# Two attention stages cut into 24 blocks of 128 destinations and one of 53, with one transfer per store

## The reference, cut to what matters

```python
h = (x @ W).reshape(n, heads, out_ch)
al_s, al_d = einsum('nhc,hc->nh', h, a_src), einsum('nhc,hc->nh', h, a_dst)
e = leaky_relu(al_s[src] + al_d[dst], 0.2)
ee = exp(e - segment_max(e, dst)[dst])
alpha = ee / (segment_sum(ee, dst)[dst] + 1e-16)
out = segment_sum(h[src] * alpha[:, :, None], dst) + b
```

## Time and profile before

| | us |
|---|---|
| median of 3 runs | 3902.7 (3895.01 to 3902.9) |
| the profiled execution, as a run | 3902.42 |
| its span, first to last instruction | 3900.3 |
| TensorE matmul busy | 3489.8 (89%) |
| TensorE weight load busy | 3228.9 (83%) |
| VectorE busy | 2067.2 (53%) |
| ScalarE busy | 1702.6 (44%) |
| GpSimd busy | 231.6 (6%) |
| line 1866 in g1a, first and last start | 1938.3 and 2512.5 |
| line 1866 in g2a, first and last start | 2668.7 and 3242.9 |

### The profile page before, as it was taken

One profiled execution on the slowest core, in us unless ns is written; L12 is line 12 of the kernel. 1 busy time (PEld: TensorE's weight loads), 2 busy tenths in 40 slices (PEclk: granted clock), 3 DMA queues, 4 the chain that ended last, 5 costly groups with the idle time before them and its releaser, 6 DMA issues. The chain is left out here.

```text
span 3900.3 us, 65697 instructions
## 1 busy us (share of the span) xinstructions
PE 3489.8 (89%) x27372; PEld 3228.9 (83%) x27372; DVE 2067.2 (53%) x2212; ACT 1702.6 (44%) x1945; POOL 231.6 (6%) x320
## 2 busy tenths in 40 slices
PE   3888889999956999878699999788999996899899
PEld 3568879999956999745599999778999996899676
DVE  6665556666653222364367667514667663466421
ACT  0444445555523434232155555414555552455332
POOL 1000000000001222100101001100011001000000
PEclk9879989999967999889799999999999998999979
DMA  3213365655525655501256555324556553654020
GB/s 110 56 33 49 52 139 150 161 159 143 143 78 173 203 188 178 161 15 32 70 150 170 146 163 154 89 80 130 145 163 170 140 153 86 161 138 137 14 56 27
DMA packets 184563, 464.88 MB, mean 119 GB/s; under 512 B 73944, under 2 KB 106465, under 8 KB 182777
## 3 DMA queue, kind: packets, MB, share of 16 engines
q1 hardware_dynamic: 166984, 424.31, 40.0%
q0 software_dynamic: 13904, 33.84, 2.8%
q10 hardware_dynamic: 3399, 2.76, 0.2%
HBM read 407.32 MB, written 53.50 MB: 118 GB/s over the span
## 5 line engine op out<-in xcount | busy, mean ns | idle before, releaser
L1866 PE MATMUL g2a_ps<-HX,g2a_x 125*125 125x129 f32 (+2 forms) x5200 | 574.5, 273 | 7.8 <-DVE g2a_x L1742 7.8
L1866 PE MATMUL g1a_ps<-HX,g1a_x 125*125 125x129 f32 (+2 forms) x5200 | 574.5, 273 | 7.8 <-DVE g1a_x L1742 7.8
L1866 PEld LDWEIGHTS g2a_ps<-HX,g2a_x 125*125 125x125 f32 x5200 | 574.3, 188 | 8.0 <-issue 8.0
L1866 PEld LDWEIGHTS g1a_ps<-HX,g1a_x 125*125 125x125 f32 x5200 | 574.3, 188 | 8.0 <-issue 8.0
L1866 PE MATMUL g0a_ps<-HX,g0a_x 125*125 125x122 f32 x5000 | 548.3, 273 | 7.9 <-DVE g0a_x L1742 7.9
L1866 PEld LDWEIGHTS g0a_ps<-HX,g0a_x 125*125 125x125 f32 x5000 | 548.1, 190 | 8.0 <-issue 8.0
L1742 DVE SCALAR_TENSOR_TENSOR g2a_x<-g2a_x,g2a_flat,g2a_ct 125x3125 f32<-125x3125 f32 x100 | 347.3, 3475 | 188.2 <-ACT g2a_x L1794 188.2
L1742 DVE SCALAR_TENSOR_TENSOR g1a_x<-g1a_x,g1a_flat,g1a_ct 125x3125 f32<-125x3125 f32 x100 | 347.3, 3474 | 188.1 <-ACT g1a_x L1794 188.1
L1742 DVE SCALAR_TENSOR_TENSOR g0a_x<-g0a_x,g0a_flat,HX 125x3125 f32<-125x3125 f32 x100 | 347.3, 3475 | 180.2 <-ACT g0a_x L1794 180.2
L1794 ACT ACTIVATE g2a_x<-g2a_grow,g2a_minus,g2a_steep 125x3125 f32<-125x3125 f32 x100 | 299.3, 2995 | 248.3 <-PE g2a_ps L1866 248.3
L1794 ACT ACTIVATE g1a_x<-g1a_grow,g1a_minus,g1a_steep 125x3125 f32<-125x3125 f32 x100 | 299.3, 2995 | 248.3 <-PE g1a_ps L1866 248.2
(11 more groups left out here) (577 smaller groups left out, 3897.0 us busy)
## 6 DMA issues: line engine op xcount, KB each, us to landing
HX<-counted SPq DMA_DIRECT2D x150, 683.6 KB
g1a_ct<-counted SPq DMA_DIRECT2D x100, 683.6 KB
g2a_ct<-counted SPq DMA_DIRECT2D x100, 683.6 KB
moe_wa<-in_L_ffn_W SPq DMA_DIRECT2D x56, 1024.0 KB
counted<-HX SPq DMA_DIRECT2D x12, 1367.2 KB
HX<-counted SPq DMA_DIRECT2D x150, 79.3 KB
g1a_ct<-counted SPq DMA_DIRECT2D x100, 79.3 KB
g2a_ct<-counted SPq DMA_DIRECT2D x100, 79.3 KB
```

Source lines behind the costliest of these rows:

```text
L1866: done = nc.tensor.matmul(ps[0:R, bank, col:col + f1 - f0], x[:, n % XR, t * R:(t + 1) * R], whole_row[:, sb, h0 + f0:h0 + f1], start=(sb ...
```

## The change

In the two stages with output "elu" the destinations are cut into 24 blocks of 128 and one of 53 (24 x 128 + 53 = 3125) in place of 25 of 125. The sources stay in 25 blocks of 125. So a weight load has 128 columns in 24 of 25 blocks, and 53 in the last; the number of matmuls and the moving operand stay. `D_` is the block's size and `rows(t)` the number of destinations in block t. The last block, the one whose columns are split over banks 0 and 1, becomes a chunk of its own for `divide`, `elu`, `lower` and the store (ND = 9 chunks, while the banks and the moves stay at CH = 8); all other chunks have three blocks. The buffers `y` and `low` hold three blocks in place of four. Each store is one transfer of 128 partitions (53 for the last chunk) in place of two of 112 and 13 partitions, so 9 x 4 = 36 transfers in a stage. The buffer `wide` is renamed `span`, because `wide` now is the flag. In the stages g0a and g3a nothing changes.

```diff
-    tiles = [range(per * c, per * c + per if c < CH - 1 else T) for c in range(CH)]
-    most = 4
+    wide = g.out == "elu"
+    D_, ND = (P, CH + 1) if wide else (R, CH)
+    tiles = [range(per * c, T if c == ND - 1 else per * c + per) for c in range(ND)]
+    most = 3 if wide else 4
...
-        raw, rec = s.sb("raw", [R, T, F + 1]), s.sb("rec", [R, T])
-        y = s.sb("y", [R, YR, most, F])
+        raw, rec = s.sb("raw", [D_, T, F + 1]), s.sb("rec", [D_, T])
+        y = s.sb("y", [D_, YR, most, F])
...
+        def rows(t):
+            return min(D_, N - D_ * t)
...
-                for n in range(G * CH):
-                    gr, c = n // CH, n % CH
-                    t0, t1 = tiles[c][0], tiles[c][-1] + 1
+                for n in range(G * ND):
+                    gr, c = n // ND, n % ND
+                    t0, t1, p = tiles[c][0], tiles[c][-1] + 1, rows(tiles[c][0])
                     pool.wait_ge(y_ready, n + 1)
-                    tile_dma(pool, OUT[t0 * R:t1 * R, gr * F:(gr + 1) * F].rearrange("(t p) f -> p t f", p=R), y[:, n % YR, 0:t1 - t0, :], y_out[n % YR])
+                    pool.dma_start(OUT[t0 * P:t0 * P + p * (t1 - t0), gr * F:(gr + 1) * F].rearrange("(t p) f -> p t f", p=p), y[0:p, n % YR, 0:t1 - t0, :]).then_inc(y_out[n % YR], 16)
                 for k in range(YR):
-                    pool.wait_ge(y_out[k], 32 * (G * CH // YR))
+                    pool.wait_ge(y_out[k], 16 * (G * ND // YR))
...
-                dve.wait_ge(moved, n + 1)
+                dve.wait_ge(moved, gr * CH + min(c + 1, CH))
...
-            for n in range(NU + XR + CH + 2):
+            for n in range(NU + XR + ND + 2):
...
-                done = nc.scalar.activation(raw[:, t0:t0 + n, :], ps[0:R, bank, 0:n * W].rearrange("p (t w) -> p t w", t=n)[:, :, b0:b0 + F + 1], ACT.Copy)
+                done = nc.scalar.activation(raw[:, t0:t0 + n, :], ps[0:D_, bank, 0:n * W].rearrange("p (t w) -> p t w", t=n)[:, :, b0:b0 + F + 1], ACT.Copy)
                 for t, col, f0, f1 in found[n:]:
-                    done = nc.scalar.activation(raw[:, t, f0:f1], ps[0:R, bank, col:col + f1 - f0], ACT.Copy)
+                    p = rows(t)
+                    done = nc.scalar.activation(raw[0:p, t, f0:f1], ps[0:p, bank, col:col + f1 - f0], ACT.Copy)
...
-                        done = nc.tensor.matmul(ps[0:R, bank, col:col + f1 - f0], x[:, n % XR, t * R:(t + 1) * R], whole_row[:, sb, h0 + f0:h0 + f1],
+                        done = nc.tensor.matmul(ps[0:rows(t), bank, col:col + f1 - f0], x[:, n % XR, t * D_:t * D_ + rows(t)], whole_row[:, sb, h0 + f0:h0 + f1],
```

More of the change, by code:

```diff
@@ L1630, in stage_gat_sums @@
             ct = spare.bitcast(BF16).rearrange("p (k n) -> p k n", k=CR)
-        raw, rec = s.sb("raw", [R, T, F + 1]), s.sb("rec", [R, T])
-        y = s.sb("y", [R, YR, most, F])
+        raw, rec = s.sb("raw", [D_, T, F + 1]), s.sb("rec", [D_, T])
+        y = s.sb("y", [D_, YR, most, F])
         if g.out == "elu":
-            low = s.sb("low", [R, 2, most, F])
+            low = s.sb("low", [D_, 2, most, F])
         ends, least, both = s.sb("ends", [R, 2 * S]), s.sb("least", [R, S]), s.sb("both", [R, 2 * S])
         end, diag, middle = s.sb("end", [2 * S, 1]), s.sb("diag", [2 * S, 2 * S]), s.sb("middle", [R, S])
-        wide, under = s.sb("wide", [1, S]), s.sb("under", [R, 1])
+        span, under = s.sb("wide", [1, S]), s.sb("under", [R, 1])
         near, far = s.sb("near", [R, S, T]), s.sb("far", [R, S, T])
@@ L1724, in prepare @@
                 nc.vector.tensor_tensor(middle[:], both[:, 0:S], both[:, S:2 * S], ALU.subtract)
-                nc.vector.tensor_tensor(wide[:], both[0:1, 0:S], both[0:1, S:2 * S], ALU.add)
+                nc.vector.tensor_tensor(span[:], both[0:1, 0:S], both[0:1, S:2 * S], ALU.add)
                 nc.vector.drain()
                 nc.vector.tensor_scalar(middle[:], middle[:], 0.5, None, ALU.mult)
-                nc.vector.tensor_reduce(wide[:, 0:1], wide[:], AX_X, ALU.max)
+                nc.vector.tensor_reduce(span[:, 0:1], span[:], AX_X, ALU.max)
                 nc.vector.drain()
@@ L1731, in prepare @@
                 nc.vector.tensor_tensor(near[:], AL[:, 0:S, :], middle[:].unsqueeze(2).to_broadcast([R, S, T]), ALU.subtract)
-                nc.vector.tensor_scalar(wide[:, 0:1], wide[:, 0:1], SPAN, None, ALU.is_gt)
+                nc.vector.tensor_scalar(span[:, 0:1], span[:, 0:1], SPAN, None, ALU.is_gt)
                 nc.vector.drain()
@@ L1735, in prepare @@
                 nc.vector.tensor_scalar(near[:], near[:], SPAN / 2, -SPAN / 2, ALU.min, ALU.max).then_inc(stepped, 1)
-                nc.vector.tensor_tensor(m.flag[:], m.flag[:], wide[:, 0:1], ALU.max)
+                nc.vector.tensor_tensor(m.flag[:], m.flag[:], span[:, 0:1], ALU.max)
             def weigh(n):
@@ L1745, in divide @@
             def divide(gr, c):
-                n, t0, t1 = gr * CH + c, tiles[c][0], tiles[c][-1] + 1
-                dve.wait_ge(moved, n + 1)
-                nc.vector.reciprocal(rec[:, t0:t1], raw[:, t0:t1, F])
+                n, t0, t1, p = gr * ND + c, tiles[c][0], tiles[c][-1] + 1, rows(tiles[c][0])
+                dve.wait_ge(moved, gr * CH + min(c + 1, CH))
+                nc.vector.reciprocal(rec[0:p, t0:t1], raw[0:p, t0:t1, F])
                 nc.vector.drain()
-                over = rec[:, t0:t1].unsqueeze(2).to_broadcast([R, t1 - t0, F])
+                over = rec[0:p, t0:t1].unsqueeze(2).to_broadcast([p, t1 - t0, F])
                 if g.out == "plain":
@@ L1753, in divide @@
                     return
-                yt = y[:, n % YR, 0:t1 - t0, :]
+                yt = y[0:p, n % YR, 0:t1 - t0, :]
                 if g.out == "elu" and n >= YR:
-                    dve.wait_ge(y_out[n % YR], 32 * (n // YR))
-                nc.vector.tensor_tensor(yt, raw[:, t0:t1, 0:F], over, ALU.mult).then_inc(divided, 1)
+                    dve.wait_ge(y_out[n % YR], 16 * (n // YR))
+                nc.vector.tensor_tensor(yt, raw[0:p, t0:t1, 0:F], over, ALU.mult).then_inc(divided, 1)
                 nc.vector.drain()
                 if g.out == "elu":
-                    nc.vector.tensor_scalar(low[:, n % 2, 0:t1 - t0, :], yt, 0.0, None, ALU.min).then_inc(low_ready, 1)
+                    nc.vector.tensor_scalar(low[0:p, n % 2, 0:t1 - t0, :], yt, 0.0, None, ALU.min).then_inc(low_ready, 1)
                 else:
@@ L1765, in elu @@
             def elu(gr, c):
-                n, t0, t1 = gr * CH + c, tiles[c][0], tiles[c][-1] + 1
-                yt = y[:, n % YR, 0:t1 - t0, :]
+                n, t0, t1, p = gr * ND + c, tiles[c][0], tiles[c][-1] + 1, rows(tiles[c][0])
+                yt = y[0:p, n % YR, 0:t1 - t0, :]
                 dve.wait_ge(low_exp, n + 1)
-                nc.vector.scalar_tensor_tensor(out=yt, in0=low[:, n % 2, 0:t1 - t0, :], scalar=-1.0, in1=yt, op0=ALU.add, op1=ALU.max).then_inc(y_ready, 1)
+                nc.vector.scalar_tensor_tensor(out=yt, in0=low[0:p, n % 2, 0:t1 - t0, :], scalar=-1.0, in1=yt, op0=ALU.add, op1=ALU.max).then_inc(y_ready, 1)
             prepare()
@@ L1780, in _ @@
                     c = n - last(gr) - XR + 1
-                    if g.out == "elu" and 0 <= c - 2 < CH:
+                    if g.out == "elu" and 0 <= c - 2 < ND:
                         elu(gr, c - 2)
-                    if 0 <= c < CH:
+                    if 0 <= c < ND:
                         divide(gr, c)
@@ L1797, in move @@
                 if gr > 0 and c == 0:
-                    act.wait_ge(divided, gr * CH)
+                    act.wait_ge(divided, gr * ND)
                 if c < CH - 1:
@@ L1804, in move @@
                 t0, n = found[0][0], len([p for p in found if p[2:] == (0, W)])
-                done = nc.scalar.activation(raw[:, t0:t0 + n, :], ps[0:R, bank, 0:n * W].rearrange("p (t w) -> p t w", t=n)[:, :, b0:b0 + F + 1], ACT.Copy)
+                done = nc.scalar.activation(raw[:, t0:t0 + n, :], ps[0:D_, bank, 0:n * W].rearrange("p (t w) -> p t w", t=n)[:, :, b0:b0 + F + 1], ACT.Copy)
                 for t, col, f0, f1 in found[n:]:
-                    done = nc.scalar.activation(raw[:, t, f0:f1], ps[0:R, bank, col:col + f1 - f0], ACT.Copy)
+                    p = rows(t)
+                    done = nc.scalar.activation(raw[0:p, t, f0:f1], ps[0:p, bank, col:col + f1 - f0], ACT.Copy)
                 done.then_inc(moved, 1)
             def lower(gr, c):
-                n = gr * CH + c
+                n, p = gr * ND + c, rows(tiles[c][0])
                 act.wait_ge(low_ready, n + 1)
-                part = low[:, n % 2, 0:len(tiles[c]), :]
+                part = low[0:p, n % 2, 0:len(tiles[c]), :]
                 nc.scalar.activation(part, part, ACT.Exp).then_inc(low_exp, 1)
@@ L1826, in _ @@
             nc.scalar.drain()
-            for n in range(NU + XR + CH):
+            for n in range(NU + XR + ND):
                 if n < NU:
@@ L1834, in _ @@
                     c = n - last(gr) - XR
```

(2 more changed lines are left out.)

## The result

| | before | after |
|---|---|---|
| median of 6 runs, us | 3899.98 (3895.01 to 3902.9) | 4009.85 (4007.71 to 4011.6) |
| span of the profiled execution, us | 3900.3 | 4007.5 |

What follows compares the result with a forecast made beforehand. TensorE was taken to set the two stages' length. 3902.42 + 3.8 (TensorE) - 2 x 0.4 (stage ends) - 2 x 2.2 (drains) = 3901.0 us, forecast as 3901; the 8-in-10 range was 3886 to 3910.

Steps and rivals of the forecast that it cites:

- The bound on TensorE: In g1a and g2a: TensorE sets the stages' length; g1a's matmuls busy 574.5 us, idle 7.8 before their first only.
- Loads of 128 columns: Full loads behind matmuls of 129 columns: 111.7 ns against 110.0, 46 per block of sources, 76.7 ns more.
- The last block, 53 columns: The last block's four instructions per block of sources: short loads save 57.5 ns, bounded from 0 to 60.
- Rival B: In each of 200 blocks of sources: short loads save nothing, all 52 steps 111.7 ns, +18.0 us, 3915.5 us; chance 0.12.
- The group's end: At group borders: TensorE runs on without a gap; VectorE's extra chunk, about 1.2 us, is hidden except in the last group.
- The stage's end and the drain: End of both stages: last store lands 0.4 us sooner, GpSimd's drain before the barrier shrinks by 2.2 us, per stage.
- Rivals A and C: A: full load hidden behind 129 moving columns, 3886 us, chance 0.14; C: GpSimd's drain stays, 3905.7 us, chance 0.12.

## Why the prediction was wrong

*The bound on TensorE* held: it sets the stages' length in the changed kernel and in the seven experiments (their matmuls in g1a and g2a leave no gap).

*Loads of 128 columns*, +76.7 ns per block of sources: right. The kernel padded to 128 runs at 111.67 ns a step against 111.7 forecast, and the one with 65 columns at 5748 ns against 5746.

*The last block, 53 columns*: this step failed, and the 110 us stand in it. It priced the two short loads by their own length, -57.5 ns, and bounded the saving from 0 to 60. Their length is as forecast (123 ns alone, closely spaced), but the step into and out of them is not one of a train. Measured over the forecast of 5738 are 551 ns per block of sources, 110 us for the 200 of both stages. The bound was wrong in kind: it took "no saving" for the worst. None of the rows showed a train that changes between wide and narrow loads, since g1a loads 125 columns throughout, and the rows of 8 and 32 columns were single loads. Where a sequence is not in the trace, its cost has to be bounded below nothing too, by a step with nothing overlapped: a matmul of 129 columns is recorded with 273 ns from start to end, 163 more than its step, and four such changes make 652 ns, or 130 us. That bound was to be had from the rows. The trace of before even has a change with its price, the load of 5 rows in the last stage, which starts 0.35 us late; it was not among the rows.

*Rival B* named the mechanism (the switch of shape exposes the load) and priced it at a full load's step, 18 us; the size was off by a factor of six. Against it were held the short single loads, which say nothing of a change.

*The group's end*: right; TensorE has no gap at the borders.

*The stage's end and the drain*: right in sum. From the last matmul's start to the next stage's first load it is 2.5 us less in g1a and 2.9 in g2a (forecast 2.6). Of its parts, the last issue comes 0.2 us later after the last matmul (forecast 0.2 earlier), and the landing is 0.5 quicker. The drain fell from 5.29 to 2.99, 83 ns for each of 64 and of 36 transfers. As a law of the number of transfers alone it is not right: 32 transfers of 125 partitions leave 1.04 us. What else it counts stays open.

*Rivals A and C* are out: 128 under 129 costs 111.67, not 110.0, and the drain did shrink.

The sum of what was measured: +117 us of TensorE and -5.4 at the ends are 111, against 110 between the medians and 107.2 between the spans. The 4 us between 111 and 107.2 are in the stages that did not change: in the two profiled executions those ahead of g1a, between g1a and g2a, and behind g2a are 1.8, 1.4 and 1.0 us shorter.

## What to carry to other kernels

Before cutting a dimension so that a small rest is left, look at the width of the rest's weight load: at 64 columns or fewer amid wide ones, each change cost 110 to 165 ns here on average, and the four together (551 ns) more than the block's own steps (379 by the forecast). Pad such a rest over the border or cut so that the rest stays wide; that took back all of the loss (65 columns, 3899.95 us, or blocks of 126, 3892.09). Putting the narrow loads side by side took back 63 of the 110 us. And choose a width by both lines, the load's and the matmul's: the widest block is not the best one once its load takes longer than the matmul it should hide behind.

## What the runs showed of the hardware

- Two lines tell the steps of wide f32 products here: 2w/2.4 + 5 ns for a load of w columns, 2m/2.4 + 2.5 for a matmul of m, the later one counts (111.67 at 128 under 129, 109.97 at 125 under 129; within 0.1 ns but for 258 moving columns, where they give 217.5 and 218.6 was measured).
- The border lies between 64 and 65 columns for the products of g1a and g2a: 4017.38 us against 3899.95. A load of 5 rows among loads of 128 waits in the same way (0.35 us), the 4-column loads of transposes do not.
- GpSimd's drain ahead of a barrier took 5.29 us behind 64 transfers, 2.99 behind 36, 1.04 behind 32 of another kind; with the stores on SyncE it was gone, and the time from the last matmul's start to the next stage 4.4 us shorter (21.4 to 17.0).
- VectorE's minimum of 384 elements takes 0.36 us, and up to 1.04 us while GpSimd issues a transfer of 125 partitions.
